# xDeepFM recommender kernel in fp32 on one core: four row copies held back, the bias row made first, the CIN folds combined on VectorE, and the last deep block computed in two halves

## What is computed

```python
emb = tables[feat_idx, sparse]                       # [512, 26, 32]
linear_out = lin_sparse_w[feat_idx, sparse].sum(-1) + dense @ lin_dense_w
for w, bb in ((conv1_w, conv1_b), (conv2_w, conv2_b)):
    hp = einsum('bhd,bmd->bhmd', xk, emb).reshape(-1, h * 26, 32)
    xn = sigmoid(einsum('oi,bid->bod', w, hp) + bb)  # 128 outputs
    xk, keep = xn[:, :64], xn[:, 64:]
cin_out = concat(keeps).sum(-1) @ cin_w + cin_b
deep: 845 -> 1024 -> 512 -> 256, tanh each; deep_out = h3 @ deep_w + deep_b
out = linear_out + cin_out + deep_out + bias
```

## Time and profile before

| | us |
|---|---|
| median of 3 runs | 432.55 (431.69 to 432.77) |
| profiled execution, whole | 432.29 |
| its span | 430.4 |
| TensorE busy | 413.3 (96% of the span) |
| VectorE, ScalarE, GpSimd busy | 320.0, 161.0, 167.3 |
| mean granted TensorE clock | 0.992 of full |

### The profile page before, as it was taken

How to read it: one execution, slowest core, us unless ns; L and a number is a source line. 1 busy time by engine, 2 the same in 40 slices (tenths; PEclk the granted TensorE clock), 3 DMA queues, 4 the chain that set the end, 5 groups by cost and what they waited for, 6 DMA issues and landing times. The chain is left out here.

```text
span 430.4 us, 5216 instructions
## 1 busy us (share of the span) xinstructions
PE 413.3 (96%) x1874; PEld 167.6 (39%) x1874; DVE 320.0 (74%) x356; ACT 161.0 (37%) x264; POOL 167.3 (39%) x146
## 2 busy tenths in 40 slices
PE   3978989999999999999999999999999999999997
PEld 1422323333333333333233333333333344886784
DVE  4115799898999799999798998998989895332121
ACT  3073252544544534535253544443543411111011
POOL 6663466664746584675540000000000193870000
PEclk9996999999999999999999999999999999999999
DMA  5357696888786898778887778675856720320000
GB/s 195 82 122 164 168 229 162 194 192 196 177 202 141 200 193 210 173 191 184 191 190 189 178 186 192 163 201 133 213 143 153 177 66 10 114 76 0 0 2 0
DMA packets 38304, 64.03 MB, mean 149 GB/s; under 512 B 19601, under 2 KB 22033, under 8 KB 38278
## 3 DMA queue, kind: packets, MB, share of 16 engines
q1 hardware_dynamic: 34694, 61.93, 58.3%
q0 software_dynamic: 3584, 1.76, 3.3%
HBM read 61.96 MB, written 1.71 MB: 148 GB/s over the span
## 5 line engine op out<-in xcount | busy, mean ns | idle before, releaser
L355 POOL DMA_INDIRECT emb<-in_table,rows x112 | 132.8, 1186 | 86.1 <-DMA emb<-in_table,rows 52.6
L730 DVE TENSOR_TENSOR prod<-ring,xk 128x1024 f32<-128x1024 f32 x112 | 132.7, 1217 | 29.2 <-PE ring L431 14.2
L730 DVE TENSOR_TENSOR copied<-copied,xk 128x1024 f32<-128x1024 f32 x96 | 115.4, 1242 | 0.5
L441 PE MATMUL conv<-prod,w_sb 128*64 128x512 f32 x448 | 112.2, 615 | 0.0
L441 PE MATMUL conv<-copied,w_sb 128*64 128x512 f32 x384 | 91.9, 594 | 1.5 <-DVE copied L730 1.5
L419 PE MATMUL conv<-sq,w_sb 117*64 117x512 f32 x384 | 88.1, 593 | 0.3 <-issue 0.3
L579 ACT ACTIVATE xk<-conv,const_sb 64x512 f32<-64x512 f32 x64 | 43.7, 683 | 97.2 <-PE conv L419 84.1
L376 POOL TENSOR_TENSOR xt_lo<-xt,xt_hi 128x512 fp32r<-128x512 f32 (+1 forms) x7 | 12.8, 1863 | 122.1 <-ACT xt_hi L640 122.1
L568 ACT ACTIVATE sq<-ring 117x512 f32<-117x512 f32 x90 | 48.6, 594 | 29.7 <-PE ring L403 23.5
L441 PEld LDWEIGHTS conv<-copied,w_sb 128*64 128x64 f32 x384 | 26.8, 137 | 57.6 <-issue 45.4
L419 PEld LDWEIGHTS conv<-sq,w_sb 117*64 117x64 f32 x384 | 27.2, 136 | 54.2 <-issue 53.4
(11 more groups left out here) (76 smaller groups left out, 299.2 us busy)
## 6 DMA issues: line engine op xcount, KB each, us to landing
copied<-laid SPq DMA_DIRECT2D x192, 256.0 KB
wpiece<-in_mlp SPq DMA_DIRECT2D x22, 256.0 KB
emb<-in_table,rows POOLq DMA_INDIRECT x112
raw<-laid SPq DMA_DIRECT2D x32, 52.0 KB
laid<-emb SPq DMA_DIRECT2D x16, 96.0 KB
sel_f<-in_sel SPq DMA_DIRECT2D x1, 832.0 KB, 5.7
const_sb<-in_const SPq DMA_DIRECT2D x1, 626.0 KB, 4.2
w_sb<-in_w SPq DMA_DIRECT2D x1, 416.0 KB, 6.3
```

The source lines that it names most:

```text
L355: pool.indirect_dma_start(out=emb[0:n, i, j, :], out_offset=None, in_=table, in_offset=bass.IndirectOffsetOnAxis(ap=rows[0:n, i, j:j + 1], ...
L441: mm = nc.tensor.matmul(conv[i % 2][c * HALF:(c + 1) * HALF, :], w2_sb[:, t, :], prod_of(r)[:, c, :], start=(t == 0), stop=(t == T2 - 1))
L730: nc.vector.tensor_tensor(prod_of(r)[:, :, :].rearrange("p c n -> p (c n)"), left[:, :, :].rearrange("p c n -> p (c n)"), xk[i % 2][:, :, ...
```

## The change

- **SP:** copies 2 and 3 wait until TensorE has done `main` of tile 0, copies 4 and 5 until it has done tile 2; pair 2's `lay_out` comes between copies 3 and 4. The dense features for `aux` are loaded before pair 0's `lay_out`.
- **POOL:** the gather of pair 1 no longer waits until pair 0's has landed.
- **Bias row:** one warm-up matmul fewer; in its place TensorE multiplies `aux` into one row of `conv[1]`, ScalarE copies it to `row_sb` ahead of pair 0's squares, and TensorE's `layer1(0, 1)`, which uses that bank, waits for the copy.
- **ScalarE:** `x_high(1)` goes ahead of the `res1` sigmoid of (0, 1).
- **Folds:** VectorE scales and adds the two halves of `fold` (two instructions of 128x256), one fp32 matmul of 256 columns sums over partitions, ScalarE copies the 2x256 result, SP moves it to one row, VectorE adds the rows before the end. The L537 and L541 matmuls between deep layers 1 and 2 are gone.
- **Last block:** deep layer 3's second block runs as two column halves of 256 in two banks, with 12 matmuls each; its tanh, the last row matmuls and the last addition are in halves too.

The diff, cut to its core ("..." for what is left out):

```diff
-WARM = 13
+WARM = 12
...
@@ sync
+            sp.wait_ge(zeroed, 1)
+            sp.dma_start(aux[DENSE_AT:DENSE_AT + ND, :], dense_t).then_inc(aux_in, 16)
             lay_out(0)
             fetch(0)
...
             for n in range(2, RC):
+                if n % 2 == 0:
+                    sp.wait_ge(main_done, n - 1)
                 copy(n)
-            lay_out(2)
+                if n == 3:
+                    lay_out(2)
             fetch(2)
-            sp.wait_ge(zeroed, 1)
-            sp.dma_start(aux[DENSE_AT:DENSE_AT + ND, :], dense_t).then_inc(dense_in, 16)
...
-            sp.wait_ge(row_read, 1)
+            sp.wait_ge(cin_copied, 1)
+            for c in range(2):
+                sp.dma_start(cin_row[0:1, :].rearrange("p (i c b) -> p c i b", c=2, b=CB)[:, c],
+                             cin2[c:c + 1, :, :]).then_inc(cin_in, 16)
+            sp.wait_ge(row_read, 2)
@@ gpsimd, gather
-                if i:
+                if i >= 2:
                     pool.wait_ge(rows_in[(i - 1) % GSEM], ROWS * ((i - 1) // GSEM + 1))
@@ tensor
+                if (i, c) == (0, 1):
+                    pe.wait_ge(aux_read, 1)
...
+            def deep_halves(layer, mt):
+                hi, lo, kt, xh, xl = deep_layers[layer]
+                n = sum(MT[:layer]) + mt
+                pe.wait_ge(tanh_done, n - 1)
+                for h in range(2):
+                    at = slice(h * BH, (h + 1) * BH)
+                    for k in range(kt):
+                        for j, (w, x_) in enumerate(((hi, xh), (lo, xh), (hi, xl))):
+                            mm = nc.tensor.matmul(half_bank[h], w[:, k, mt * P:(mt + 1) * P],
+                                                  x_[:, k, at], start=(k == 0 and j == 0),
+                                                  stop=(k == kt - 1 and j == 2))
+                    mm.then_inc(mlp_done, 1)
...
+            pe.wait_ge(aux_in, 16)
+            nc.tensor.matmul(conv[1][0:1, :], small_sb[:, C_AUX:C_AUX + 1], aux[:, :], start=True, stop=True)\
+              .then_inc(aux_done, 1)
...
+                    pe.wait_ge(cin_step, 2)
+                    nc.tensor.matmul(cin_ps, small_sb[:, C_ONE:C_ONE + 2], fold[:, 0, :, :], start=True, stop=True)\
+                      .then_inc(cin_done, 1)
+            deep_halves(2, MT[2] - 1)
+            pe.wait_ge(l2_read, NPAIR)
+            pe.wait_ge(tanh_done, HT - 1)
+            for h in range(2):
+                nc.tensor.matmul(row_half[h], small_sb[:, C_DEEP:C_DEEP + 1], h3[:, 0, h * BH:(h + 1) * BH],
+                                 start=True, stop=False)
+            for h in range(2):
+                pe.wait_ge(tanh_done, HT + h)
+                nc.tensor.matmul(row_half[h], small_sb[:, C_DEEP + 1:C_DEEP + 2],
+                                 h3[:, 1, h * BH:(h + 1) * BH], start=False, stop=True).then_inc(row_done, 1)
@@ scalar
+                if between is not None:
+                    x_high(between)
...
+            act.wait_ge(aux_done, 1)
+            nc.scalar.activation(row_sb[:, :], conv[1][0:1, :], ACT.Copy).then_inc(aux_read, 1)
...
-            sigmoid(0, 1)
-            x_high(1)
+            sigmoid(0, 1, 1)
@@ vector
+            nc.vector.tensor_scalar(fold[:, 0, :, :], fold[:, 0, :, :], small_sb[:, C_CIN1:C_CIN1 + 1], None,
+                                    ALU.mult).then_inc(cin_step, 1)
...
+            nc.vector.scalar_tensor_tensor(fold[:, 0, :, :], fold[:, 1, :, :], small_sb[:, C_CIN2:C_CIN2 + 1],
+                                           fold[:, 0, :, :], ALU.mult, ALU.add).then_inc(cin_step, 1)
...
+            nc.vector.tensor_tensor(lin_row[:, :], lin_row[:, :], row_sb[:, :], ALU.add).then_inc(row_step, 1)
...
+            nc.vector.tensor_tensor(lin_row[:, :], lin_row[:, :], cin_row[:, :], ALU.add).then_inc(row_step, 1)
...
+            for h in range(2):
+                at = slice(h * BH, (h + 1) * BH)
+                dve.wait_ge(row_done, h + 1)
+                nc.vector.tensor_tensor(row_sb[:, at], row_half[h], lin_row[:, at], ALU.add).then_inc(row_read, 1)
```

More of the change, by code:

```diff
@@ L182, in build @@
         HT = sum(MT)
+        BH = B // 2
+        cin_ps = ring[2][0:2, 0, 0:NPAIR * CB]
+        half_bank = [MLP_BANKS[(HT - 1) % 2][:, 0:BH], ring[1][:, 0, 0:BH]]
+        row_half = [row_ps[0:1, 0:BH], ring[2][0:1, 1, 0:BH]]
         def piece(k):
@@ L528, in _ @@
                 pe.wait_ge(piece_lo, (KW, KW + K2, PIECES)[layer])
-                for mt in range(1 if layer == 0 else 0, MT[layer]):
+                for mt in range(1 if layer == 0 else 0, MT[layer] - (1 if layer == 2 else 0)):
                     deep(layer, mt)
                 if layer == 0:
-                    pe.wait_ge(fold1_done, NPAIR)
-                    pe.wait_ge(fold2_done, NPAIR)
-                    pe.wait_ge(dense_in, 32)
-                    pe.wait_ge(l2_read, NPAIR)
-                    nc.tensor.matmul(row_ps[0:1, :], small_sb[:, C_AUX:C_AUX + 1], aux[:, :], start=True, stop=False)
-                    by_c = row_ps[0:1, :].rearrange("p (i c b) -> p c i b", c=2, b=CB)
-                    for k, col in enumerate((C_CIN1, C_CIN2)):
-                        for c in range(2):
-                            nc.tensor.matmul(by_c[:, c], small_sb[:, col + c:col + c + 1],
-                                             fold[:, k, :, :], start=False, stop=False, skip_group_check=True)
-            for k in range(D3 // P):
-                pe.wait_ge(tanh_done, HT - D3 // P + k + 1)
-                mm = nc.tensor.matmul(row_ps[0:1, :], small_sb[:, C_DEEP + k:C_DEEP + k + 1], h3[:, k, :],
-                                      start=False, stop=(k == D3 // P - 1))
-            mm.then_inc(row_done, 1)
+                    pe.wait_ge(cin_step, 2)
[11 more added lines that the diff above has]
+                                 h3[:, 1, h * BH:(h + 1) * BH], start=False, stop=True).then_inc(row_done, 1)
         @block.scalar
@@ L569, in squares, with sigmoid @@
                       .then_inc(sq_done, 1)
-            def sigmoid(i, c):
+            def sigmoid(i, c, between=None):
                 bank = l1_bank(i, c)
@@ L598, in _ @@
             act.wait_ge(zeroed, 1)
-            nc.scalar.activation(row_sb[0:1, 0:1], aux[0:1, 0:1], ACT.Sigmoid)
+            nc.scalar.activation(row_sb[0:1, 0:1], aux[0:1, 0:1], ACT.Sigmoid).then_inc(table_set, 1)
             act.wait_ge(const_in, 16)
@@ L646, in _ @@
             for layer, bias in enumerate((C_B1, C_B2, C_B3)):
-                for mt in range(MT[layer]):
+                for mt in range(MT[layer] - (1 if layer == 2 else 0)):
                     act.wait_ge(mlp_done, n + 1)
@@ L654, in _ @@
                     n += 1
+                if layer == 0:
+                    act.wait_ge(cin_done, 1)
+                    nc.scalar.activation(cin2[:, :, :], cin_ps.rearrange("p (i b) -> p i b", b=CB),
+                                         ACT.Copy).then_inc(cin_copied, 1)
+            for h in range(2):
+                at = slice(h * BH, (h + 1) * BH)
+                act.wait_ge(mlp_done, HT + h)
+                nc.scalar.activation(h3[:, 1, at], half_bank[h], ACT.Tanh,
+                                     bias=small_sb[:, C_B3 + 1:C_B3 + 2]).then_inc(tanh_done, 1)
         @block.vector
@@ L764, in _ @@
                     n += 1
-            dve.wait_ge(row_done, 1)
+            dve.wait_ge(aux_read, 1)
             dve.wait_ge(lin_in, 16)
-            nc.vector.tensor_tensor(row_sb[:, :], row_ps[0:1, :], lin_row[:, :], ALU.add).then_inc(row_read, 1)
+            nc.vector.tensor_tensor(lin_row[:, :], lin_row[:, :], row_sb[:, :], ALU.add).then_inc(row_step, 1)
+            dve.wait_ge(row_step, 1)
+            dve.wait_ge(cin_in, 32)
+            nc.vector.tensor_tensor(lin_row[:, :], lin_row[:, :], cin_row[:, :], ALU.add).then_inc(row_step, 1)
+            dve.wait_ge(row_step, 2)
+            for h in range(2):
+                at = slice(h * BH, (h + 1) * BH)
+                dve.wait_ge(row_done, h + 1)
+                nc.vector.tensor_tensor(row_sb[:, at], row_half[h], lin_row[:, at], ALU.add).then_inc(row_read, 1)
 def kernel(r_dense, r_sparse, L0_rec_tables, L0_rec_lin_sparse_w, L0_rec_lin_dense_w, L0_rec_conv1_w,
```

19 lines of the change are left out of this document (15 added, 4 removed).

## The result

The changed kernel is **slower**: 435.16 us (431.51 to 435.67, six runs) against 432.35 us for the kernel before, measured beside it (431.45 to 433.6, six runs). The ratio is 1.0066 [1.0038, 1.0095]. The forecast was 430.2, range 428.7 to 432.4. The profiled execution took 435.24 us with a span of 433.4, 3.0 more than before, and its mean granted clock was 0.984 instead of 0.992.

The account below looks back on a forecast made before the run. TensorE was taken to bound the main part, so gains come only ahead of it, behind it or by removing matmuls. The terms -2.16 - 0.12 + 0.2 - 0.3 = -2.4 us gave 430.2 against 432.55, range 428.7 to 432.4.

Parts of the forecast that it names:

- Between the deep layers: Bias and fold matmuls leave TensorE's chain, one fp32 matmul of 256 columns is added: 2.16 us less.
- The tail: Last deep block in halves 0.14 us more, last addition 0.26 less; together 0.12 us less.
- rival (a): Last block's halves bound by weight loads, 0.225 us a matmul: 432.7, no change; chance 0.13.
- The row copy: At the start, ScalarE's copy of the bias row delays pair 0's squares: 0.2 us more.
- The semaphore stall: Tile 9's product waited 2.61 us on a TensorE semaphore; that may not come again: 0.3 us less.
- Rival (c): The start gains more because less copy traffic from 29 to 41 us shortens waits: 428.7; chance 0.09.
- `x_high` ahead of `res1`: At the start, brings nothing, since x_low(1) stands behind two products on VectorE whatever ScalarE does.
- For the same reason the earlier gather of pair 1 is worth nothing: At the start, no gain from the gather, since x_low(1) stands behind two products on VectorE anyway.
- The held copies. Price: nothing: Copies 2 to 5 of pair 0 held: later fetch(2) still has 2.7 us of cover, so no cost.
- Rival (b): Pair 2's raw lands late behind the held copies and TensorE waits: 434 to 438; chance 0.05.
- Sum: Terms for deep layers, tail, start and held copies give -2.4 us: 430.2 against 432.55.

Follow-up runs that it names:

- f3: Changed kernel with only POOL's wait before the gather of pair 1 put back: 0.9948 of before, 429.74 us.
- f4: The changed kernel run again, on the same chip as f3: 1.0046 of before, 432.44 us.
- e1: Changed kernel with the old order of copies, copies 2 to 5 not held: 0.9957 of before, 429.62 us.
- f1: e8 with POOL's wait before the gather of pair 1 taken out: 1.0011 of before, 431.56 us.
- g1: e4 with POOL's wait before the gather of pair 1 taken out: 1.0005 of before, 431.87 us.
- e8: Changed kernel with copies not held, row copy behind pair 0's squares, gather wait and x_high(1) as before: 0.9933 of before, 429.00 us.
- e4: Kernel before with only the end changed (folds, half blocks), bias matmul behind the fold matmul: 0.9966 of before, 429.85 us.
- f2: e8 with x_high(1) ahead of the res1 sigmoid of (0, 1): 0.9943 of before, 428.33 us.
- e2: Kernel before with nothing but the held copies: 1.0057 of before, 433.78 us.
- e10: e8 with the held copies back in: 0.9961 of before, 429.77 us.
- e6: Changed kernel with copies not held and the bias row copied behind pair 0's squares: 1.0023 of before, 432.81 us.
- e3: Changed kernel with ScalarE's bias row copy moved behind pair 0's six squares: 0.9994 of before, 430.70 us.
- G: Marks kernels in which pair 1's gather does not wait for pair 0's; alone on the kernel before (e9) 1.0002.
- e12: e6 with copies 0 and 1 sent only when pair 0's squares are done: 1.0030 of before, 431.90 us.
- e9: Kernel before with only POOL's wait before the gather of pair 1 taken out: 1.0002 of before, 430.67 us.
- e11: e10 with pair 3's lay_out two copies earlier and its fetch ahead of copies 10 and 11: 0.9951 of before, 428.71 us.

## Why the prediction was wrong, point by point

Two terms of the sum had been put at nothing and were not: the gather of pair 1, whose cost is shown on one chip by one line (f3, f4), and the held copies, whose cost depends on what stands beside them. With the gather's line back and everything else as changed, the kernel is at 0.9948 (f3), 2.2 us faster than before, where the forecast had 2.4.

- **Between the deep layers** (-2.16): right, 2.16 by the chain, and no wait at the head of layer 2.
- **The tail** (-0.12): right, 0.14 less. The pitch of a half matmul is 2.87 / 24 = 0.120 us, forecast 0.121. So rival (a) fell. The Trainium skill, "TensorE: Matmul & The Clock Gate", section "Part 3: Packing small matmuls — row/col tiling", has the rule that loads overlap only where row groups differ. The trace disagrees at 256 columns too: load and stream one after the other would be 0.216, an estimate from the figures of that page of the Trainium skill, and 0.120 was measured. The same section also lets a load go ahead when it targets a background weight buffer, and a load beside the stream is what the pitch shows; the prediction left that half of the section out. Behind the block it was 2.52 us and is 431.84 - 429.57 = 2.27, 0.25 less, for which I had 0.26, but not as I had put it: both halves of the addition stand on the chain (0.78), and what shrank is TensorE's part (0.52 + 0.43 + 0.45 = 1.40 for 1.82), because the last two passes lie beside the first half of the addition.
- **The row copy** (+0.2): no more than that. The first square starts 0.66 us behind the first matmul of the sums in f3, e1 and the changed kernel, which have the copy ahead of it, and 0.53 behind it in the kernel before (22.70 against 22.17): 0.13 more. In e1 pair 0's first product is 0.14 us later than before.
- **The semaphore stall** (-0.3): tile 9, which stood behind the 2.61 us wait of the earlier trace rows, came some 2.7 us sooner against tile 8 in 17 of the 19 other profiles, and 0.95 and 1.6 sooner in f1 and g1. So it was an accident of that execution, not something that the change removes. It was worth 0.86 us at pair 1's first product (e8). What is left of it at the end cannot be told: at the last pair's first product e8 is 0.25 us ahead of the kernel before, and e4, which has the old start too, 1.97. Rival (c), a start that gains more from less copy traffic, is not seen either: no kernel with held copies is faster than its like without them beyond the intervals.
- **`x_high` ahead of `res1`** (nothing): right, f2.
- **"For the same reason the earlier gather of pair 1 is worth nothing"**: this step failed. I had asked only who waits for the gather, and not what it runs beside once it is not held back. It costs 2.7 us in the changed kernel by the medians (f4 432.44, f3 429.74) and 4.2 by the ratios (0.98% of 431). The profiles show late releases at pair 0's squares, a later `fetch(0)` and longer stretches at 1.2 GHz in such kernels; that these make up the whole cost is my reading and was not tested. It had no rival, and no term but zero.
- **"The held copies. Price: nothing"**: this failed too. What I worked out came true: copies at 38.24 (forecast 37.8), `fetch(2)` at 46.54 (46), `x_high(2)` ended at 52.1 (51.1), TensorE had no wait from it. Rival (b) watched the wrong pair. Two MB of copies moved into 38 to 51 us meet the copies that follow them, and the one that pays is pair 3, whose `lay_out` is issued at 53.5. With the gather's wait in place that is worth 0.57%, 2.5 us, on the kernel before (e2), but only 0.28% in e10 against e8 and 0.05% in f3 against f2, both with overlapping intervals. Without the wait, e1 (0.9957) lies well below the changed kernel (1.0046 to 1.0066, not on its chip), but e6, without held copies, is no better than e3 with them. So the delay of pair 3 is shown, and its price in the whole time is not one number.
- **Sum.** With the end at -2.3, the kernel without both parts (e8) is 2.9 us faster than before by its ratio [1.7, 4.1], against my -2.4. The forecast was right for the rest of the change and left out costs that are larger than its gain. The bounds that it gave its own case were a little off as well: the low end of the terms it names is 429.6 and not 429.3, the high end 431.4 and not 431.2, and the tail's low end is 0.3 less and not 0.4. That changes nothing in the outcome.

**What stays open.** Why releases come late with G at pair 0's squares, and how far the late `fetch(0)` and the late releases have one cause. The rows show that the gathers of two pairs and copies 0 and 1 are then on their way together, but e12, which should have parted them, changed too much else, and f1's DMA share from 20 to 25 us (0.92) is not far from e8's (0.86). Nor is it shown why e9, the kernel before with G, does without the loss, nor what the further 1.5 us are that the changed kernel's profile loses between the first products of pairs 7 and 8. In pair 8 TensorE waited another 1.1 us for a product of a copied tile (at 216.66).

## What to carry over

When transfers are held back, draw up the queue for the pair after the next as well: the backlog is paid by the first small transfer that is issued behind it, here 96 KB behind 2 MB. A wait that nothing seems to need may still keep other work in time, as POOL's did here for a reason that is not shown. Taking one away deserves a run inside the full change, several times repeated: in the kernel before, alone, it cost nothing that could be measured (e9). The fold and half-block edits were worth 2.3 us on the chain, and the version with the lowest ratio keeps them, the bias matmul at the start and the old order of everything else there (e8, 0.9933 [0.9904, 0.9961]); f2, f3, e10 and e11 are not apart from it.

## What the runs showed of the hardware that I had not expected

- With one wait of POOL ahead of a pair's indirect gathers dropped, TensorE's releases of ScalarE at pair 0's squares came 0.8 to 2.4 us late in seven of twelve profiles, and in none of eight with the wait, though the gather was issued only 1.3 us sooner. Executions under 0.992 went from 7 of 74 to 61 of 120 (e12 apart).
- Such a late release also occurs with the wait in place, and then several updates come together: four updates of `main` within 0.18 us, the first of them 3.4 us behind its last matmul (kernel before, 51.44).
- 128x128 weight loads go on beside the stream at 256 columns: 0.120 us a matmul, against 0.230 at 512; one after the other they would be 0.11 + 0.115 = 0.225, an estimate from the earlier trace rows.
- With the DMA share at 1.05, one write of 96 KB, one of 8 KB and the two reads of 52 KB behind them took 68.38 - 53.14 = 15.2 us from the first issue to ScalarE's use (e10), and 64.12 - 54.46 = 9.7 in the kernel before.
